# Spreading B and C by DMA instead of by TensorE, with the product with B on GpSimd, in a selective-scan and mixture-of-experts kernel

## The reference

```
xc    = causal_conv4(in_proj_w @ ctx);  u = silu(xc + conv_b)
dt_lo, Bm, Cm = split(x_proj_w @ u, [8, 16, 16])
delta = softplus(dt_proj_w @ dt_lo + dt_proj_b);  A = -exp(A_log)
for each token l:                      # state: 256 channels x 16
    state = state * exp(delta[l] * A) + (delta[l] * u[l]) * Bm[l]
    y[l]  = sum over the 16 states of state * Cm[l]
x1 = x + (y + D * u) * silu(layernorm(x));  xs = layernorm(x1)
gates = softmax(xs @ router_w + router_b), best 6 of 32, normalised
out = x1 + mean of 2 shared experts + sum of gates * expert_e(xs)
```

## Time and profile before

| | us |
|---|---|
| median of 3 runs | 418.9 (418.45 to 421.33) |
| the profiled execution | 418.02 |
| its span | 416.2 |

### The profile page before, as it was taken

The page is one execution under the profiler, slowest core; times in us unless marked ns, Lnnn a source line. Parts: engine busy times, 40 slices in busy tenths (PEclk is TensorE's granted clock), DMA queues, the critical chain, the costliest instruction groups (busy, mean ns, idle before and its releaser), DMA issues.

```text
span 416.2 us, 7115 instructions
## 1 busy us (share of the span) xinstructions
PE 374.5 (90%) x2383; PEld 334.5 (80%) x2383; DVE 307.5 (74%) x527; ACT 214.8 (52%) x478; POOL 119.2 (29%) x88
## 2 busy tenths in 40 slices
PE   4555668579999999989999999999999999999996
PEld 3334456468899998878999988888999989999996
DVE  3499997689899955899899666998995634444443
ACT  3777534456544436546543437555432335666672
POOL 0555442003333300023334000133432003535442
PEclk8659889869999999999999999999999999999999
DMA  7343460034686321546764222576753226767520
GB/s 229 90 139 104 109 220 25 5 127 146 204 225 178 110 63 52 180 136 205 236 187 123 75 71 81 161 205 204 204 179 97 58 71 223 238 192 217 166 72 27
DMA packets 37456, 58.62 MB, mean 141 GB/s; under 512 B 5778, under 2 KB 15284, under 8 KB 37428
## 3 DMA queue, kind: packets, MB, share of 16 engines
q1 hardware_dynamic: 37428, 58.27, 46.6%
HBM read 57.06 MB, written 1.18 MB: 140 GB/s over the span
## 4 chain that ended last, share of the span: by engine, by line
PE 76%; DVE 15%; issue 6%; ACT 1%; DVEq 1%; ACTq 0%
PE acc L491 34%; PE z L510 10%; PE z L511 9%; PE z L512 9%; DVE bu L728 5%; DVE bu L721 3%; PE z L425 2%; PE acc L391 2%; PE bb L406 1%; PE cc L415 1%; PE acc L496 1%; DVE stage L822 1%; PE misc L452 1%; PE cc L440 1%; PE bb L433 1%
## 5 line engine op out<-in xcount | busy, mean ns | idle before, releaser
L643 ACT ACTIVATE z<-z,par 128x256 f32<-128x256 f32 x188 | 76.3, 443 | 137.3 <-PE z L512 137.3
L491 PE MATMUL acc<-stage,w 128*128 128x256 f32 x564 | 134.8, 382 | 0.0
L510 PE MATMUL z<-xh,w1l 128*128 128x256 f32 (+1 forms) x376 | 120.2, 320 | 0.0
L491 PEld LDWEIGHTS acc<-stage,w 128*128 128x128 f32 x564 | 102.8, 191 | 12.2
L873 POOL TENSOR_TENSOR ya<-ya,pr 128x512 f32<-128x512 f32 x42 | 54.9, 1307 | 187.9 <-DVE pr L739 187.9
L512 PE MATMUL z<-xh,w1h 128*128 128x256 f32 (+1 forms) x376 | 107.1, 285 | 0.0
L511 PE MATMUL z<-xl,w1h 128*128 128x256 f32 (+1 forms) x376 | 107.0, 285 | 0.0
L728 DVE TENSOR_TENSOR_SCAN bu<-dA,bu 128x512 f32<-128x512 f32 x64 | 78.7, 1240 | 1.7
L510 PEld LDWEIGHTS z<-xh,w1l 128*128 128x128 f32 x376 | 72.0, 191 | 4.9 <-issue 3.1
L511 PEld LDWEIGHTS z<-xl,w1h 128*128 128x128 f32 x376 | 72.0, 191 | 1.6
L512 PEld LDWEIGHTS z<-xh,w1h 128*128 128x128 f32 x376 | 72.0, 191 | 0.0
(11 more groups left out here) (113 smaller groups left out, 390.6 us busy)
## 6 DMA issues: line engine op xcount, KB each, us to landing
w<-in_w SPq DMA_DIRECT2D x92, 256.0 KB, 3.3
gone<-gates SPq DMA_DIRECT2D x64, 256.0 KB, 3.8
stage<-in_w SPq DMA_DIRECT2D x11, 512.0 KB, 3.6
grem<-gates SPq DMA_DIRECT2D x96, 48.0 KB, 3.1
xr<-in_xr SPq DMA_DIRECT2D x4, 256.0 KB, 4.2
x<-in_xT SPq DMA_DIRECT2D x4, 256.0 KB, 3.9
grem<-gates SPq DMA_DIRECT2D x32, 32.0 KB, 2.7
out<-x SPq DMA_DIRECT2D x4, 256.0 KB, 3.8
```

Source lines behind the costliest of these rows:

```text
L491: mm = pe.matmul(acc[:, k, :], weights, h, start=t + k + n == 0, stop=last, skip_group_check=True)
L510: pe.matmul(z[p % ZB][:, i, :], w1l[:, t, one], xh_, start=k == 0, stop=False)
L643: ins = act.activation(z[p % ZB][:, i, :], z[p % ZB][:, i, :], ACT.Relu, bias=b1[:, t:t + 1])
```

## The change

- The 40 rows of x_proj (dt, B, C) are copied to SBUF as `xd` by one ScalarE instruction. SyncE writes B and C to a DRAM scratch `bc` (`spill_bc`) and reads each chunk back with a broadcast over 128 partitions (`load_bc`: one DMA of 256 KB for B into `bt`, one for C into `ct`, a ring of four chunks each, in the bytes that `w2l` and `w2h` use in batch 3). The matmuls L406 and L415, `selbc` and the step "split" are gone.
- The step "bu" goes from VectorE to GpSimd, and one pair earlier in `UNITS`.
- `dA` lies in two PSUM tiles (one for each k). The scan writes its states over the decays in PSUM; "prod" reads them there. A ScalarE copy of two zeros per unit is added, and the decays of a unit now wait for the "prod" of two units before rather than for its scan.
- W1 is staged in three slots of `grem` (whose own loads wait for the last piece), `hg` has a buffer of its own, and the pieces are spread: after `usig`, `dtl`, `sp`, after chunks 1, 3, 5 and 7, one more in `HEAD`, four in `OPEN`.
- In `HEAD`, scan and prod alternate (scan 0, prod 0, scan 1, prod 1) where before both scans came first.

```diff
 for _c in range(NC):
-    UNITS += [(("B", _c), 2 * _c), (("C", _c), 2 * _c + 1)]
     for _k in range(KD):
         _u = 2 * _c + _k
-        UNITS += [(("decay", _c, _k), max(_u - 1, 0)), (("bu", _c, _k), _u), (("scan", _c, _k), _u),
+        UNITS += [(("decay", _c, _k), max(_u - 1, 0)), (("bu", _c, _k), max(_u - 1, 0)), (("scan", _c, _k), _u),
                   (("prod", _c, _k), _u), (("fold", _c, _k), _u)]
...
-    HEAD += [(("scan", _c, _k), 0) for _k in range(KD)]
-    HEAD += [(("C", _c), 0)] + [(("prod", _c, _k), 0) for _k in range(KD)] + [(("piece", _c), 0)]
+    for _k in range(KD):
+        HEAD += [(("scan", _c, _k), 0), (("prod", _c, _k), 0)]
+    HEAD += [("piece", 0)] if _c in (1, 3, 5, 7) else []
...
-OPEN = [[("gates", 0), ("turn", 0)],
-        [(n, 1) for n in (("B", 0), ("C", 0), ("decay", 0, 0), ("decay", 0, 1), ("bu", 0, 0), ("scan", 0, 0), ("prod", 0, 0))],
+OPEN = [[("gates", 0), ("turn", 0), ("piece", 0)],
+        [(n, 1) for n in (("decay", 0, 0), ("bu", 0, 0), ("decay", 0, 1), ("bu", 0, 1), ("scan", 0, 0), ("prod", 0, 0), "piece")],
...
+            def load_bc(b, c):
+                if b * NC + c >= BRING:
+                    eng.wait_ge(S["prod_done"], (b * NC + c - BRING + 1) * KD)
...
+                for row, dst, ld in ((2 * c, bt, ld_b), (NS + 2 * c, ct, ld_c)):
+                    eng.dma_start(dst[:, c % BRING], bc_d[b % 2, row:row + 2, :].rearrange(
+                        "(o n) l -> o n l", o=1).broadcast_to([P, 2, L])).then_inc(ld[c % BRING], 16)
...
                     if c:
-                        act.wait_ge(S["scan_done"], (b * NC + c - 1) * KD + k + 1)
+                        act.wait_ge(S["prod_done"], (b * NC + c - 1) * KD + k + 1)
...
+                    act.activation(dA[k][:, :, 0:1], zeros, ACT.Copy)
...
-                    dve.tensor_tensor_scan(bu[:, k, :], dA[:, k, :], bu[:, k, :], 0.0, ALU.mult,
+                    dve.tensor_tensor_scan(flat(dA[k]), flat(dA[k]), bu[:, k, :], 0.0, ALU.mult,
...
+                elif name[0] == "bu":                       # GpSimd's list
+                    c, k = name[1:]
+                    g = (b * NC + c - 1) * KD + k + 1
+                    if c == 0:
+                        pool.wait_ge(S["delta_done"], b + 1)
+                    if c or not first(b):
+                        pool.wait_ge(S["scan_done"], g)
+                    wait_bc(pool, ld_b, b, c)
+                    pool.tensor_tensor(bu[:, k, :].rearrange("p (j l) -> p j l", j=2), bt[:, c % BRING],
+                                       du[:, k:k + 1, :].broadcast_to([P, 2, L]), ALU.mult).then_inc(S["bu_done"], 1)
```

More of the change, by code:

```diff
@@ L29 @@
 NREM = NR * REM // P
-NBC = 3 * 2 * NS
+NBC = 2 * NS
 NXA = NBC + DR
@@ L36 @@
 NW = -(-NT // WCH)
+WRING = 3
+BRING = 4
 PAR = {}
@@ L128, in xattn_ffn_kernel @@
         w2 = sb("w2", [P, RING, 2, DX])
+        with nc.sbuf_tensor("bt", [P, BRING, 2, L], F32) as bt, nc.sbuf_tensor("ct", [P, BRING, 2, L], F32) as ct:
+            pass
         w2l = sb("w2l", [P, 4, 2, DX], F32R)
@@ L149, in xattn_ffn_kernel @@
         epsc = sb("epsc", [P, 1])
+        zeros = sb("zeros", [P, 2, 1])[:]
         st6 = sb("st6", [P, KD, 6])
@@ L341, in gate_rem @@
                     eng.dma_start(grem[at:at + n, t, :], gates_d[b % 2, e:e + 1, :].broadcast_to([n, L])).then_inc(ld_rem, 16)
-            load_xr(1)
+            for i in range(3):
+                load_w1(i)
+            eng.dma_start(ctxT[:, 1], ctx_d[:, 1]).then_inc(ld_ctx, 16)
+            spill_bc(0)
+            for c in range(BRING):
+                load_bc(0, c)
+                if c in (1, 3):
+                    load_w1(3 + c // 2)
+            for c in range(BRING, NC):
+                load_bc(0, c)
+                if c in (5, 7):
+                    load_w1(5 + c // 6)
+            for p in range(RING):
+                load_w2(p)
+            load_xr(1)
+            load_w1(7)
+            load_w1(8)
+            spill_bc(1)
+            for c in range(BRING):
+                load_bc(1, c)
+            load_w1(9)
+            load_w1(10)
             for b in range(B):
@@ L352, in _ @@
                 for p in range(NP):
+                    if b == 0 and p == 0:
+                        load_w1(NW - 1)
+                    if 0 < b < B - 1 and 0 < p < BRING:
+                        load_bc(b + 1, p)
+                    if b < B - 1 and p in (4, 6, 8, 10):
+                        load_bc(b + 1, BRING + (p - 4) // 2)
+                    if b + 2 < B and p == NP - 2:
+                        spill_bc(b + 2)
+                    if b + 2 < B and p == NP - 1:
+                        load_bc(b + 2, 0)
                     if SINGLE0 <= p < SINGLE0 + NSINGLE - GRING:
@@ L355, in _ @@
                         gate_one(b, p + GRING)
+                    if b == 0 and p == 4:
+                        eng.wait_ge(w1l_done, NW)
                     if 4 <= p < 4 + REMPARTS:
@@ L395, in step @@
             def step(name, b):
[L396 to L418, removed]
+                if name[0] == "sum":
                     sum_states(name[1])
@@ L430, in step @@
                         pe.wait_ge(ld_ctx, 16 * b)
-                        pe.wait_ge(S["bu_done"], NC * KD)
+                        if not (type(b) is int and b == 1):
+                            pe.wait_ge(S["gates_done"], b - 1)
                     for k in range(KD):
-                        mm = pe.matmul(xin(b)[:, k, :], win[:, k * P:(k + 1) * P], ctxT[:, b % 2, :], start=True, stop=True)
+                        mm = pe.matmul(misc[:, k, :], win[:, k * P:(k + 1) * P], ctxT[:, b % 2, :], start=True, stop=True)
                     mm.then_inc(S["xin_done"], 1)
@@ L437, in step @@
                         pe.wait_ge(ld_par, 32)
+                    else:
+                        pe.wait_ge(S["prod_done"], b * NC * KD)
                     pe.wait_ge(S["u_done"], b + 1)
                     for k in range(KD):
-                        mm = pe.matmul(cc[0:NXA, 0, :], xall[:, k, :], u[:, k, :], start=k == 0, stop=k == KD - 1)
+                        mm = pe.matmul(xdt[0:NXA, 0, :], xall[:, k, :], u[:, k, :], start=k == 0, stop=k == KD - 1)
                     mm.then_inc(S["xall_done"], 1)
@@ L638, in pair @@
             def pair(b, p, beside):
-                if first(b) and p < SKEW:
-                    act.wait_ge(w1l_done, NW)
                 act.wait_ge(S["z_ready"], b * NP + p + 1)
@@ L878, in step @@
                                            ALU.add).then_inc(S["y_folded"], 1)
-                elif first(b) and name in ("usig", "dtl", "sp"):
-                    split_w1(1)
-                elif name == "rest":
-                    split_w1(len(todo))
             def pair(b, p, beside):
@@ L964 @@
     out = nc.dram_tensor("out_0", (P, KD, B, L), F32, kind="ExternalOutput").ap()
+    bc = nc.dram_tensor("bc", (2, 2 * NS, L), F32).ap()
     gates = nc.dram_tensor("gates", (2, NR, L), F32).ap()
-    xattn_ffn_kernel(nc, *args, gates, out)
+    xattn_ffn_kernel(nc, *args, bc, gates, out)
     r = run_bass_kernel_spmd(nc, [arrays], core_ids=[0])
```

138 lines of the change are left out of this document (58 added, 80 removed).

## The result

| | before | after |
|---|---|---|
| median us (range, runs) | 420.12 (418.45 to 422.16, 4) | 476.77 (475.69 to 480.97, 4) |
| ratio after / before | | 1.137, 95% interval 1.129 to 1.144 |
| profiled execution, its span | 418.02, 416.2 | 480.97, 479.2 |

The changed kernel is 57 us slower. 476 us was forecast.

The account below looks back on a forecast made before the run. TensorE bounds the kernel beside the experts before; after, a loop through GpSimd and VectorE at 4.83 us per unit. With head, opening and batches 52.4 us later and 6 for the clock, 418.0 + 52.4 + 6 = 476 us; range 452 to 495.

Parts of the forecast that it names:

- The loop: Units of batches 1 to 3: fold, bu, scan, prod wait in turn on GpSimd and VectorE, 4.83 us; chance 0.75.
- 11 + 13 + 13 turns: Loop turns beside the units of batches 1, 2 and 3, 4.83 us each; thirteen turns make 62.8 us.
- fold 15 to the mean: End of each batch's units: 6.05 us to the end of x1, the mean some 0.1 us behind it.
- mean to fold 2: Start of batches 2 and 3: three pairs without spreading, but bu 2 waits for its load; 0.4 us gained.
- The load of chunk 1: Batches 2 and 3: issued only after the second layer in pair 0, lands 3.8 us later; bu 2 waits.
- The clock: TensorE stands still some 8 us before each mean; three stops at 2 us each, 6 us in all.
- The opening: After the head: GpSimd's pieces, bu and a fold take 15.9 us from about 86.3; unit 4's scan at 105.6.
- The head: Batch start on VectorE: waits in chunks 1, 2, 4 and 6; ends at 63.7 us, 4.0 us later.
- The signs: Profile after, beside the units: VectorE idle about 1.5 us per unit for bu, TensorE busy about 65%, folds 4.8 us apart.
- The loop turns faster: Rival: fold and bu overlap on GpSimd or releases are shorter, 4.3 us per turn, 456 us; chance 0.08.
- TensorE binds at the lower clock: Rival: at 1.2 GHz a pair takes up to 6.3 us; half the turns so, 498 us; chance 0.1.
- TensorE stays the bound, 406: Rival: GpSimd hands over bu early enough for 3.17 us per unit, so the change gains, 406 us; chance 0.04.

Follow-up runs that it names:

- another order: Changed kernel with the bu of unit u + 1 in front of the fold of unit u in GpSimd's list; 414.3 us, ratio 0.986.
- a shorter fold: Changed kernel with GpSimd's fold working on 8 of the 512 columns, order and waits kept; 435.9 us, ratio 1.041.
- the early load: Changed kernel with chunk 1 of the next batch's B and C loaded at pair 23, with chunk 0; 471.9 us, ratio 1.124.
- both: Changed kernel with bu in front of the fold on GpSimd and chunk 1 of B and C loaded at pair 23; 408.4 us, ratio 0.973.
- the best kernel: Changed kernel with bu before fold, chunk 1 loaded at pair 23, and rs1 and the W1 piece halves moved in `HEAD`; 404.6 us, ratio 0.966.

## Why the prediction was right

**The loop.** Its terms were 0.86 + 1.25 + 1.30 + 0.09 + 1.33 = 4.83 and measured 0.85 + 1.23 + 1.27 + 0.03 + 1.34 = 4.72. The largest misses are 0.03 for bu and 0.06 for the release, which had no row and was taken from the middle of its bounds. The scan that writes over PSUM takes 1229 ns on average, and 1.23 in the earlier trace rows from SBUF: no difference, as taken. By the rule of the Trainium skill's "VectorE: DVE Perf Modes", section on the TRN2 errata, the turn would have been 4.90, as estimated; this trace shows no such step. Over 37 turns the loop was 3.8 us cheaper than summed. That the chain is the cause is shown three ways: another order takes it away (414.3), a shorter fold shortens it by just the fold (435.9), and each engine waits 90 us for the other.

**Against its own stages,** in the profiled execution. With the forecast span of 476 - 1.8 = 474.2:

| | forecast | measured | difference |
|---|---|---|---|
| head, first mean | +4.0 | 65.1 to 69.1 | 0 |
| fold 4 of batch 1 | 107.9 | 111.76 | +3.9 |
| 11 + 13 + 13 turns | 178.7 | 52.2 + 61.7 + 61.0 | -3.8 |
| fold 15 to the mean, three | 6.15, 6.15, 6.13 | 6.23, 6.23, 5.04 | -0.9 |
| mean to fold 2, batches 2, 3 | 33.9 each | 39.16, 37.33 | +8.7 |
| last mean to the end | 96.0 | 98.5 | +2.5 |
| clock | 6.0 | in the rows above | -6.0 |

That is +4.4 of the +5.0 us measured; most of the rest is rounding in the forecast, whose stages add up to 474.8. The mechanism, the loop, was right, and its size to 0.11 us a turn. That the total came within 1 us is luck: the loop was 3.8 us cheaper than summed and the load of chunk 1 4.5 us dearer, and the two cancel. The third way from fold 15 to the mean is 1.1 us short, since the hg in front of y on VectorE, which waited 2.43 us for ScalarE before the change, waits no more.

- **The load of chunk 1 was undersized.** Batches 2 and 3 were allowed 3.8 us from the second layer in pair 0, which left about 0.3 us of wait. Measured, bu waited 7.34 and 6.14 us for it. The step took the gates' loads for the duration only, and did not ask where in SyncE's list the load stands: four loads of gates and one of W2 are issued in front of it, and it landed 5.0 us after its issue, not 3.8. With the early load, mean to fold 2 takes 35.74 and 36.25, so the load cost 3.4 and 1.1 us.
- **The clock was sized well.** With the early load, mean to fold 2 is 2.0 and 2.5 us more than the 33.7 that the kernel before leaves without the spreading (34.4, from its mean at 146.06 to 180.48, less 3 x 0.23), and last mean to end is 2.5 more in the changed kernel: 7.0 for three stops, forecast 6.0. The stops are 8.46, 8.47 and 7.13 us, forecast some 8. This is a difference of stages, and no run takes the stops away alone, but the best kernel has the same steps there. Behind its mean at 225.06, with a stop of 0.20 us and a granted clock of 1.00, mean to fold 2 took 33.5 us. Behind its mean at 140.83, with a stop of 1.83 us and a clock of 0.73 in the 3.2 us after it, it took 35.2. Its last mean to its end took 96.7. Against these the three stops cost 2.3, 2.8 and 1.8, together 6.8.
- **The opening** was 3.9 late in this execution, but 0.6 in the one with the early load (fold 4 at 108.50), whose kernel has the same instructions up to there. Of the 3.3 between them, 1.2 lie in front of the first mean (69.1 and 67.9) and 2.1 between it and fold 4. The 2.1 come from a meeting of two engines: a piece on GpSimd and VectorE's products of two inputs from SBUF. In the profiled execution after, the piece began at 70.80 and the squaring 0.04 us behind it. With the early load the piece began at 70.21, 0.5 us behind the squaring and 0.09 us ahead of the product that follows. After, then with the early load:

```profile
70.84 2.85 DVE L783 TENSOR_TENSOR pr<-ya 128x512 f32<-128x512 f32 x1
```

```profile
69.69 0.69 DVE L784 TENSOR_TENSOR pr<-ya 128x512 f32<-128x512 f32 x1
70.30 2.84 DVE L726 TENSOR_TENSOR u<-cv,e 128x512 f32<-128x512 f32 x1
```

In both, one product waited out the piece, 2.16 us longer than alone. After, TensorE's second mean waited for it as well: its four matmuls started at 73.74 and took 2.09 us, where with the early load they started at 70.43 and took 1.13. The 3.3 us are most of the 4.2 by which the profiled execution lies above its median, if the others went as the one with the early load; they have no profile.

**The head** came out at 63.3 for its last prod, forecast 63.7, with the waits in chunks 1, 2, 4 and 6 as told. They are 1.49, 0.55 and 2.26 us, and in chunk 6 1.16 behind a product (L764) of 1.63 that the sum had not counted: 7.1 for 8.6. The first scan was 0.56 late (24.46 for 23.9), and a unit takes 1.96 us for the 1.95 of a chunk of 3.9. The exact +4.0 at the first mean belongs to this execution: in the runs with the order, the early load, both and the thin fold, whose heads have the same instructions, the mean stands at 67.9, 67.9, 67.6 and 68.2, 2.5 to 3.1 later than before the change. So the head was summed about 1 us too long, and the opening too short: with the early load, first mean to fold 4 took 40.6 us, forecast 38.8. L764 is `sz` times `ez` (which lies in `cv`), two inputs from SBUF, and stood beside a piece; before the change it took 0.69.

**The signs.** Two of them were off. VectorE idles for 2.1 us per unit and not 1.5: a turn of 4.72 less scan 1.34 and prod and hg of 0.6 each is 2.2, which the forecast of the sign had not worked out. TensorE is busy for 75, 79 and 81% beside the units of batches 1, 2 and 3 and not 65%; why its busy time per unit is 3.5 us and more for some 3.1 stays open.

**The rivals.** "The loop turns faster" (4.3 us) did not come. "TensorE binds at the lower clock" did not come: the clock beside the units was 0.97 to 1.00, at 46 to 50 of 61 or 62 us busy. "TensorE stays the bound, 406" named as its condition the bu in front of the fold. With that order the time is 414.3. With the load and the head mended as well, it is 404.6; the prediction had priced the head's waits, at 4 us in all, and the load's at 0.3 us a batch.

**The gain that was there.** In the best kernel TensorE is at 90%, and five folds of batch 3 in a row come 3.16 us apart (276.96 to 289.60; 3.21 on average over its last 13 units), which the earlier trace rows had only for pairs without spreading (3.17; with it 3.40). The forecast 11.0 us for 48 pairs may be most of the 13.9 us between 404.6 and 418.5; no run separates it from the rest. The loads are not quite covered at this pace: GpSimd waits for a chunk of B five times, 7.2 us in all and 3.4 at most, where in the changed kernel it waited for chunk 1 only. TensorE stands still for 1.9 us for hg and for 2.6 in front of the means.

## What to carry to other kernels

When work moves to a second engine, write down the turn: what each engine's list has in front of the instruction that the other waits for. If two instructions that alternate there wait on each other's results, the pitch is the sum of both engines' times, however idle both look; the one that feeds the other engine has to stand first. Then look up where a new load stands in its queue, not only how long it takes, and give VectorE at most one input from SBUF wherever GpSimd works beside it.

## What the runs showed of the hardware that was not expected

- A VectorE product with both inputs in SBUF takes 0.68 us alone and 1.39 to 1.47 beside a GpSimd add of 128 x 512; two that began 0.04 and 0.09 us behind a GpSimd subtraction of 128 x 1024 took 2.85 and 2.84. Scan and prod with one input in PSUM show nothing of it: 1223 and 692 ns in the run with order and early load, whose GpSimd is busy for 199 us.
- GpSimd suffers as well: its product takes 1.79 us on average beside such a VectorE, for 1.28. In the run with order and early load a piece that began 0.07 us behind a VectorE product took 2.83 us for 2.36, and the product 0.68: the one that began first kept its time.
- A scan over 512 columns takes 1.23 us with decays and result in PSUM, as with both in SBUF.
- GpSimd's adds and products of 128 x 512 take 1.27 to 1.30 us, 1.23 to the next one; of 128 x 8 0.20 us, 0.16 to the next one. The release from GpSimd to VectorE takes 0.03 us.
